# The second feed-forward bias as one more row of the down product, with newly written step orders

## What is computed

```python
# block 1, a state space layer
u = silu(conv4(x @ in_w + in_b) + conv_b)            # 256 inner channels
delta = softplus((u @ dt1_w + dt1_b) @ dt2_w + dt2_b)
h = exp(delta * A) * h + expansion * B * u           # scan over tokens, 16 states
y = (sum_n C_n h_n + D * u) * silu(x @ gate_w + gate_b)
x = layernorm(x + y @ out_w + out_b)
# block 2, two layers
for l in range(2):
    q, k, v = split(shift_token(x) @ wqkv[l])        # 8 heads of 64
    x1 = x + local_attention(rotate(l2norm(q)), rotate(l2norm(k)), v) @ wo[l]
    a, g = split((layernorm(shift_token(x1)) * ln_g + ln_b) @ w1[l] + b1[l])
    x = x1 + (a * gelu(g)) @ w2[l] + b2[l]           # 341 hidden channels
x = layernorm(x_block1 + x)
```

## Time and profile before

| | before |
|---|---|
| median of 3 runs | 1025.17 us (1023.71 to 1028.51) |
| the profiled execution | 1025.69 us, its span 1023.9 us |
| PE busy | 906.2 us, 89% |
| DVE busy | 890.3 us, 87% |
| ACT busy | 788.3 us, 77% |
| POOL busy | 701.1 us, 68% |
| granted TensorE clock, mean | 0.98 of full speed |

### The profile page before, as it was taken

How to read it: one execution, slowest core, us unless ns; L and a number is a source line. 1 busy time by engine, 2 the same in 40 slices (tenths; PEclk the granted TensorE clock), 3 DMA queues, 4 the chain that set the end, 5 groups by cost and what they waited for, 6 DMA issues and landing times. The chain is left out here.

```text
span 1023.9 us, 26019 instructions
## 1 busy us (share of the span) xinstructions
PE 906.2 (89%) x10152; PEld 550.7 (54%) x10152; DVE 890.3 (87%) x1244; ACT 788.3 (77%) x1901; POOL 701.1 (68%) x386
## 2 busy tenths in 40 slices
PE   3767678999988898999899989999899999999985
PEld 1333335456455465646564555546565566676664
DVE  7798997999879997999899998999899997774643
ACT  4467766996888859977898759995987987778771
POOL 4062424998579984799588892999478497886651
PEclk9979889999999999999999999999999999999998
DMA  7000000000001100000101100100110000010000
GB/s 239 11 17 16 12 1 21 23 19 15 17 17 27 27 23 16 18 22 22 32 18 27 22 12 22 28 23 6 28 32 23 2 23 22 17 33 18 17 22 11
DMA packets 22618, 25.63 MB, mean 25 GB/s; under 512 B 2869, under 2 KB 14815, under 8 KB 22495
## 3 DMA queue, kind: packets, MB, share of 16 engines
q1 hardware_dynamic: 22207, 23.81, 9.0%
q10 hardware_dynamic: 288, 0.14, 0.0%
HBM read 9.26 MB, written 2.10 MB: 11 GB/s over the span
## 5 line engine op out<-in xcount | busy, mean ns | idle before, releaser
L1088 DVE TENSOR_TENSOR_SCAN scan<-du,decay 128x1028 f32<-128x1028 f32 (+1 forms) x160 | 315.0, 2004 | 2.8 <-issue 1.3
L793 POOL TENSOR_TENSOR rn<-ssc,expo 128x16 f32<-128x16 f32 x64 | 214.6, 3354 | 5.3
L884 ACT ACTIVATE decay<-delta,negA 128x1024 f32<-128x1024 f32 (+1 forms) x160 | 154.9, 997 | 43.3 <-DVE scan L1088 37.7
L1278 PE MATMUL YY<-scan,diag 64*64 64x512 f32 (+1 forms) x1280 | 148.1, 552 | 32.1 <-DVE scan L1088 31.7
L789 POOL TENSOR_SCALAR ssc<-ss 128x16 f32<-128x16 f32 x64 | 61.9, 967 | 152.7 <-DVE ss L1145 152.0
L798 POOL TENSOR_TENSOR qkc<-qkc,qks 128x1024 f32<-128x1024 f32 x64 | 163.0, 2547 | 0.5 <-DVE qks L1163 0.3
L802 POOL TENSOR_TENSOR qkc<-qkc,rn 128x1024 f32<-128x1024 f32 x64 | 143.5, 2242 | 5.0
L940 ACT ACTIVATE prob<-AA,nmax 128x128 f32<-128x128 f32 x240 | 84.5, 384 | 15.1 <-DVE nmax L1183 15.0
L940 ACT ACTIVATE prob<-BB,nmax 128x128 f32<-128x128 f32 x232 | 81.7, 381 | 17.3 <-DVE nmax L1183 14.9
L1145 DVE TENSOR_REDUCE ss<-sq 128x16 f32<-128x1024 f32 x64 | 77.2, 1206 | 15.1 <-ACT sq L903 15.1
L1278 PEld LDWEIGHTS YY<-scan,diag 64*64 64x64 f32 x1280 | 38.3, 139 | 94.5 <-DVE scan L1088 68.9
(11 more groups left out here) (210 smaller groups left out, 2279.2 us busy)
## 6 DMA issues: line engine op xcount, KB each, us to landing
v_even<-v_odd SPq DMA_DIRECT2D x96, 128.0 KB, 2.3
x<-in_x SPq DMA_DIRECT2D x6, 256.0 KB, 3.3
wqkv<-in_wqkv SPq DMA_DIRECT2D x1, 1536.0 KB
xT<-in_xT SPq DMA_DIRECT2D x6, 256.0 KB, 2.7
out<-outb SPq DMA_DIRECT2D x6, 256.0 KB, 2.3
w<-in_w SPq DMA_DIRECT2D x1, 682.0 KB
xT<-in_xT SPq DMA_DIRECT2D x4, 128.0 KB, 2.5
x<-in_x SPq DMA_DIRECT2D x4, 128.0 KB, 2.9
```

Source lines behind the costliest of these rows:

```text
L793: pool.tensor_tensor(rn[:, q % 2, :], ssc[:, :], expo[:, 0:2 * HEADS], ALU.pow).then_inc(rn_sb, 1)
L884: act.activation(decay[:, at % A_RING, both(g), 1:], delta[:, both(g), :], ACT.Exp, scale=negA[:, n:n + 1]).then_inc(decay_sb, 1)
L1088: dve.tensor_tensor_scan(state, step, a, 0.0, ALU.add, ALU.mult).then_inc(scan_sb, 1)
L1278: return pe.matmul(dst, lhsT, rhs, start=start, stop=stop, skip_group_check=True)
```

## The change

The array w2 gets b2 as its row 342, and the one transfer that loads the last chunk of both layers takes 86 rows in place of 85. The tile hid is filled with ones in its last chunk at the start; gelus and hidden write rows 0 to 84 of it, so row 85 stays one. In `down` the last chunk has 86 rows, and the product contains the bias. gelus 0 waits once for the signal that stands behind the fill. POOL's addition of b2, its signal and both waits for it are gone; `residual` is left for layer 1 alone, ten steps in place of twenty. b2 leaves the row table bv. All five orders and both bank tables are written anew; each holds the same steps as before but for the ten dropped residual steps.

```diff
-for _name, _n in (("A_log", NST), ("out_b", D), ("qk_scale", LAYERS * 2 * DH), ("b2", LAYERS * D)):
+for _name, _n in (("A_log", NST), ("out_b", D), ("qk_scale", LAYERS * 2 * DH)):
...
-                             (w2[0:CH[2][1], :, 2, :], t["w2"][:, 2 * P:HID, :].rearrange("l p n -> p l n"))]:
+                             (w2[0:CH[2][1] + 1, :, 2, :], t["w2"][:, 2 * P:HID + 1, :].rearrange("l p n -> p l n"))]:
...
             pool.memset(qkT[:, :, :, 0:WIN], 0.0)
+            pool.memset(hid[:, NCH - 1, :], 1.0)
             pool.memset(v_even[:, :, :], 0.0).then_inc(zeros_late, 1)
...
                 rows = x2[:, 0:tiles_of(g), :]
-                pool.tensor_tensor(rows, rows, row("b2", g, l), ALU.add).then_inc(xb2_sb, 1)
-                if l == 1:
-                    pool.wait_ge(xb2_sb, f + 1)
-                    pool.tensor_tensor(rows, rows, x1[:, g % X_RING, 0:tiles_of(g)], ALU.add).then_inc(xb1_sb, 1)
+                pool.tensor_tensor(rows, rows, x1[:, g % X_RING, 0:tiles_of(g)], ALU.add).then_inc(xb1_sb, 1)
...
             def gelus(f):
                 l, g = QUAD[f]
+                if f == 0:
+                    act.wait_ge(zeros_late, 1)
...
                 dve.wait_ge(w2_ps, f + 1)
-                dve.wait_ge(xb2_sb, f + 1)
...
                     for c, (lo, n) in enumerate(CH):
+                        n += c == NCH - 1
                         ins = mm(one("down", f)[:, i * D:(i + 1) * D], hid[0:n, c, i * P:(i + 1) * P], w2[0:n, l, c, :],
...
-        "wqkv": f["wqkv"], "wo": f["wo"], "w1": f["w1"], "w2": f["w2"], **_consts()}
+        "wqkv": f["wqkv"], "wo": f["wo"], "w1": f["w1"], "w2": np.concatenate([f["w2"], f["b2"][:, None, :]], 1), **_consts()}
```

Of the orders, the piece around the last scan on PE, before and after:

```diff
-state_y 9 10, weighted 49, norm_T 13, scores 50, state_y 9 11, up_gate 13, state_y 9 12, state_y 9 13, state_y 9 14,
-up_a 13 0, qk_in 52, state_y 9 15, out_T 49, probs_T 50, up_a 13 1, mamba_out 9, qk_T 51, weighted 50, up_a 13 2,
...
+9, layer_T 0 8, state_y 9 10, state_y 9 11, qk_T 50, scores 50, qk_in 52, norm_T 13, state_y 9 12, state_y 9 13,
+state_y 9 14, v_in 51, weighted 49, state_y 9 15, probs_T 50, v_in 52, out_T 49, mamba_out 9, up_gate 13, up_a 13 0,
```

and the piece around the eighth group's step size on DVE:

```diff
-attended 41, row_max 42, hidden 11 0, differences 8, hidden 11 1, inverse 42, hidden 11 2, rope 44, sums 44,
-step_size 8, ffn_sum 11, scan 8 0, attended 42, scan 8 1, row_max 43, scan 8 2, scan 8 3, rope 45, inverse 43, scan
...
+11 1, inverse 42, conv0 8, mamba_norm 7, conv1 8, hidden 11 2, rope 44, sums 44, step_size 8, differences 8, ffn_sum
+11, rope 45, row_max 43, attended 42, scan 8 0, sums 45, scan 8 1, scan 8 2, scan 8 3, scan 8 4, row_max 44, inverse
```

More of the change, by code:

```diff
@@ L95 @@
[L95 to L109, removed]
@@ L303 @@
[L303 to L306 removed]
+0, mamba_norm 0, conv0 1, conv1 1, sums 0, rope 0, differences 1, rope 1, step_size 1, sums 1, scan 1 0, scan 1 1,
@@ new lines @@
+attended 7, row_max 8, rope 10, scan 3 12, attn_sum 2, sums 10, scan 3 13, inverse 8, scan 3 14, ffn_stats 2, scan 3
+15, row_max 9, gated 3, attended 8, rope 11, mamba_sum 3, inverse 9, ffn_norm 2, conv0 4, mamba_norm 3, conv1 4,
+sums 11, differences 4, row_max 10, attended 9, hidden 2 0, sums 12, inverse 10, rope 12, hidden 2 1, attended 10,
+row_max 11, step_size 4, sums 13, hidden 2 2, rope 13, scan 4 0, ffn_sum 2, attn_sum 3, scan 4 1, inverse 11, sums
+14, row_max 12, rope 14, attended 11, inverse 12, ffn_stats 3, scan 4 2, rope 15, sums 15, ffn_norm 3, row_max 13,
@@ new lines @@
+6 1, row_max 23, hidden 6 2, attended 22, rope 25, sums 25, scan 5 9, inverse 23, ffn_sum 6, scan 5 10, scan 5 11,
+attended 23, row_max 24, rope 26, sums 26, inverse 24, scan 5 12, scan 5 13, scan 5 14, attn_sum 7, scan 5 15, sums
+27, ffn_stats 7, row_max 25, attended 24, gated 5, rope 27, mamba_sum 5, ffn_norm 7, row_max 26, inverse 25,
+final_stats 2, attended 25, mamba_norm 5, conv0 6, conv1 6, hidden 7 0, row_max 27, final_out 2, sums 28, rope 28,
+inverse 26, attended 26, hidden 7 1, differences 6, hidden 7 2, sums 29, rope 29, inverse 27, step_size 6, ffn_sum
@@ new lines @@
+attended 32, rope 35, ffn_norm 9, final_stats 3, gated 6, inverse 33, attended 33, row_max 34, mamba_sum 6, hidden 9
+0, final_out 3, mamba_norm 6, conv0 7, conv1 7, row_max 35, rope 36, sums 36, differences 7, hidden 9 1, hidden 9 2,
+inverse 34, attended 34, sums 37, rope 37, ffn_sum 9, inverse 35, step_size 7, scan 7 0, attended 35, rope 38,
+row_max 36, sums 38, scan 7 1, scan 7 2, attn_sum 10, scan 7 3, row_max 37, inverse 36, ffn_stats 10, scan 7 4, rope
+39, attended 36, scan 7 5, ffn_norm 10, sums 39, row_max 38, scan 7 6, scan 7 7, inverse 37, inverse 38, attended
@@ new lines @@
+46, step_size 9, rope 49, scan 9 0, scan 9 1, inverse 47, scan 9 2, sums 49, scan 9 3, final_stats 5, row_max 48,
+scan 9 4, attended 47, sums 50, rope 50, scan 9 5, scan 9 6, inverse 48, scan 9 7, scan 9 8, scan 9 9, attn_sum 13,
+row_max 49, ffn_stats 13, attended 48, scan 9 10, scan 9 11, rope 51, scan 9 12, ffn_norm 13, scan 9 13, scan 9 14,
+row_max 50, sums 51, scan 9 15, final_out 5, inverse 49, attended 49, gated 9, sums 52, mamba_sum 9, inverse 50,
+rope 52, hidden 13 0, hidden 13 1, hidden 13 2, row_max 51, ffn_sum 13, attended 50, mamba_norm 9, sums 53, rope 53,
```

458 lines of the change are left out of this document (225 added, 233 removed).

## The result

| | before | after |
|---|---|---|
| median | 1026.84 us (4 runs, 1023.71 to 1029.07) | 1041.01 us (4 runs, 1040.92 to 1043.49) |
| ratio to before | | 1.0146, 95% interval 1.0111 to 1.0181 |
| the profiled execution | 1025.69 us, span 1023.9 us | 1040.92 us, span 1039.1 us |

The changed kernel is slower by 14 us, 1.5% (by the interval 1.1 to 1.8%). The forecast was 1023.7 us and no measurable change, with 1010 to 1036 as its range; the time lies above the range, and beyond the upper end of rival B (1036.9). The prediction was wrong.

The account below looks back on a forecast made before the run. DVE was taken to bound the kernel up to the last scan, PE behind it. 1025.7 - 1.6 + 4.8 - 3.2 - 2.0 = 1023.7 us, no measurable change, with a range of 1010 to 1036 us.

Parts of the forecast that it names:

- rival B: Tail and in-order stalls at attended make it slower, 1033.9 to 1036.9 us; last scan beyond 850 us; chance 0.26.
- What bounds the kernel: DVE is the bound up to the last scan, with 64.3 us idle; PE is the bound behind it.
- Part 1, the additions: Dropping POOL's b2 additions saves only DVE time they blocked, at two places: 1.6 us, bounds 0 and 1.6.
- Parts 2 and 3: Extra row in the down product, its memset, and the remaining layer-1 additions with SP's copies cost 0 us.
- Part 4, the tail: Three PE steps fall behind the last scan, where PE is the bound: +4.8 us, bounds 0 and 4.8.
- Part 4, the relief: 4.8 us less PE work ahead of the last scan gives back half of DVE's 6.4 us idle: -3.2 us.
- Part 4, the softplus: Delta waits for softplus fall 4 us, mostly groups 4 to 6; group 8 adds 2: -2 us, bounds -7 and +3.
- Part 4, attention: Softmax cover grows 7.1 to 10.7 us, attended's shrinks 8.3 to 6.0: net 0, bounds -5 and +6.
- A: New orders take 13.5 us off DVE's idle time, giving 1015.4 us; last scan before 835; chance 0.36 together with C.

Follow-up runs that it names:

- run with three steps moved: Kernel before's orders with the added bias row, attended 9, row_max 43 and mamba_norm 8 moved in DVE's order: 1026.66 us, ratio 0.9986.
- the doubled additions: Kernel before with every b2 addition on POOL done a second time into a spare tile: 1038.21 us, ratio 1.0094.
- the fills: Kernel before with a constant written into a spare tile on POOL ahead of each b2 addition: 1033.31 us, ratio 1.0054.
- the additions in the new orders: Changed kernel's orders and bank tables with all twenty b2 additions back on POOL instead of the bias row: 1055.23 us, ratio 1.0254.
- the row in the old orders: Changed kernel's bias row with the kernel before's orders and bank tables, only the ten layer-0 residual steps dropped: 1027.91 us, ratio 1.0004.
- the doubled quads: Old orders with added row, up_gate and up_a computed twice behind the last scan: quad 14 1030.41 us; quads 14, 15 and 16 1034.14 us.
- quad 13 doubled: Old orders with added row, up_gate 13 and up_a 13 0 to 2 computed twice around the last scan: 1029.88 us.
- quad 14 doubled: Old orders with added row, up_gate 14 and up_a 14 0 to 2 computed twice behind the last scan: 1030.41 us.
- moving either step sooner: Changed kernel with tile 45's sum of squares and group 9's step size both moved sooner in DVE's order: 1044.77 us, ratio 1.0165.

## Why the prediction was wrong, step by step

**What bounds the kernel.** This was the root of it. I took DVE as the bound up to the last scan, since it idles 6.4 us behind 640 us. PE was busy 197.2 of 206 us in the same window, and I didn't weigh it. And DVE's busy time has time in it in which POOL holds it. The very row with which I began the reading is one: the last scan took 3.22 us, from 843.93 to 847.15, beside a step of the rotation,

```profile
843.59 2.48 POOL L798 TENSOR_TENSOR qkc<-qkc,qks 128x1024 f32<-128x1024 f32 x1
```

and after the change, with no rotation beside it, 1.22:

```profile
855.22 1.22 DVE L1086 TENSOR_TENSOR_SCAN scan<-du,decay 128x514 f32<-128x514 f32 x1
```

The same 1244 instructions were busy between 875.7 and 901.3 us in the kernels here. The run with three steps moved shows that such time can be taken off DVE with no gain, in a stretch that PE fills. Added, it is paid: the doubled additions, the fills and the additions in the new orders made DVE busy 11.0, 4.7 and 14.4 us longer and cost 9.6, 5.5 and 11 to 14. The loop of scans is a loop of four engines in which PE and DVE are both near full, and a share of busy time doesn't say which one is late.

**Part 1, the additions (-1.6).** The bounds were 0 and 1.6. In the old orders no gain is seen (1.0004), though the interval, from 1.8 us faster to 2.7 slower, doesn't quite exclude 1.6. The Trainium skill's rule ("SBUF — State Buffer", "Who interferes with whom") agrees with what the runs show in kind: rotations beside scans hold them, rotations beside steps that read a bank don't. By its own reading the additions could have been worth up to their 26.9 us; they were worth nothing that can be told in one order and 11 to 14 in the other, and the order decides. I looked for holds only beside the additions, and so missed those beside the rotation, which stand all over the trace. The mean cover of 22 us for the rotated keys didn't speak for each tile either: in the changed kernel PE waited 2.5 us for those of tile 45.

**Parts 2 and 3 (0).** Right as far as the runs tell: 274 ns for 86 rows, and the row in the old orders is level with before.

**Part 4, the tail (+4.8).** The direction was right, and the size near: 5.9 us by the profiles. PE is busy 5.5 us longer in it. At the rates that the doubled quads paid by the medians that is 3.6 to 4.0 us, by the stretches 4.8 to 5.5 (my estimate); what is left, 0.4 to 2.3 us, would be the sequence of the steps within the tail. The tails of the old orders differ by as much (175.2 to 177.4 us with the row), so no run tells how the 5.9 divide.

**Part 4, the relief (-3.2).** This is the step that failed. Less PE work ahead of the last scan does relieve (quad 13 doubled there costs 2.0 us), but I took half of DVE's idle time as given back by the amount of work, and beyond the softplus and two covers of attention I put the new sequence at nothing. What came is +9.3. DVE's idle time grew by 24.7 us where it was to fall by 3.2, and 8 us of that lie ahead of scan 4 15, 6 in the groups 5 to 7, 10 behind. The relief itself can be seen in group 9, where the three PE steps stood:

```profile
784.80:847.10 62.30, 60.37 (x699) 37.01 (x697) 60.87 (x90) 54.99 (x139) 46.12 (x28) 1.00 0.07 17
```

and after

```profile
795.40:856.40 61.00, 55.22 (x706) 35.72 (x706) 56.97 (x89) 46.68 (x132) 38.51 (x24) 0.94 0.04 10
```

PE is busy 5.2 us less, and the stretch is 1.3 us shorter; the rest became idle time of PE. Over the whole way to the last scan PE was to be busy 4.8 us less and is busy 750.1 us against 748.1. In windows of 32 us from 192 us to the last scan its clock was 1.00 throughout before and below it in three of after (0.95, 0.95, 0.89), which is 6.7 us of full speed at most. That could make the difference, but it isn't shown: with the row in the old orders, the same PE work took 750.1 us of busy time in one profile (quad 14 doubled) and 754.6 in another (the row alone).

**Part 4, the softplus (-2.0).** The half on groups 4 to 6 was right: the delta waits there fell from 6.8 to 1.3 us, for the 4 that I took; with two new ones in the first groups, 7.2 became 2.7 over all. The wait in group 8 didn't come. Whether the time gained by it isn't shown; DVE's idle time as a whole grew.

**Part 4, attention (net 0).** I weighed two covers, the softmax's and attended's. The first held (rden ahead of the last scan 2.8 to 1.0 us), the second cost 4.7 us, within its bound of 6. The failure is in the pairs for which I made no cover at all: row_max behind scores (5.3 to 12.0 us), mamba_sum behind mamba_out (3.6 to 10.2), attn_sum behind attn_out (0.5 to 5.0). That makes 18 of the 25 us of added idle time.

**The rivals.** B named the right side, and its mark, a last scan beyond 850 us, is what came (856.4). Its mechanism, attended standing too close, is a fifth of DVE's added idle time, so B's side came in the main by another way than the one it named. What A hoped for came too (13 us less waiting for ACT, 15 us less busy time of DVE), but not its mark, a last scan before 835 us.

**What stays open.** What in the new orders makes the 9 us behind scan 7 15. By the stretches they lie in group 8 (4.9 us, with the wait for the keys of tile 45 in it) and in the tail (5.9), and not in group 9, where PE waits for the step size; moving either step sooner didn't mend them. How much is the bank tables'. What the lower clock costs by itself. The new orders with the old banks, and the three PE steps moved alone across the last scan, weren't tried.

## What to carry to other kernels

Where an order is written out by hand or by a planner for a given set of steps, taking a step out and writing new orders are two changes: time them apart, here nothing that can be told and +14 us. Before you call an engine the bound by its busy share, compare the durations of like instructions; what is longer than its like is waiting in disguise, and taking it away gained nothing here where another engine filled the stretch. Give the same weight to the next fullest engine of the stretch, here PE. When you compare two orders, make the cover of every pair of producer and consumer, not only of those that wait today.

## What the hardware showed that I had not expected

A rotation on POOL (two instructions with two operands in SBUF, 2.35 and 1.90 us) stretched instructions of DVE that work on SBUF alone, by nearly its own length: two normalisations that take 0.59 us took 4.22 with the row in the old orders, and one scan of 1.2 us took 3.2. It goes both ways (the same rotation took 2.83 + 2.71 us beside five scans). Steps that read a bank beside it kept their length (two of rope 1.23 and 1.22 us, for 1.21 elsewhere). A fill on POOL, which reads nothing, left scans alone and held a convolution step of one operand in SBUF to its end (3.40 us for 0.54).

Where PE had been busy only 1.41 and 1.23 of 4 us in a dense stretch of the changed kernel (one wait of 2.5 us, and two of 2.0 and 1.8), the granted clock was 0.57 and 0.50 over the next 4 us. And the spread of one and the same kernel goes with the clock: every run of the kernel before with a span of up to 1023.7 us had a mean clock of 0.979 or more, every one from 1027.9 us on 0.973 or less. Which of the two is the cause, these runs don't tell.
